# Coattention: the entry's own share of the output in float16 parts

## The reference, cut to what matters

```python
cq = einsum('bcd,bqd,d->bcq', c, q, w_cq) + b_cq
s = (c @ w_c + b_c)[:, :, None] + (q @ w_q + b_q)[:, None, :] + cq
a = softmax(s, axis=2)
c2q_att = einsum('bcq,bqd->bcd', a, q)
b_att = softmax(max(s, axis=2), axis=1)
q2c_att = einsum('bc,bcd->bd', b_att, c)[:, None, :]
x = concatenate([c, c2q_att, c * c2q_att, c * q2c_att], axis=-1)
z = x @ W_l.T + b_l          # added to the residual
```

## Time and profile before

| what | value |
|---|---|
| runs, median of 3 | 2402.48 us (2394.66 to 2403.4) |
| profiled execution | 2401.25 us |
| its span | 2399.5 us |
| TensorE busy in the span | 2083.1 us (87%) |
| VectorE, ScalarE, GpSimd busy | 1568.1, 1270.4, 1097.1 us |
| mean granted TensorE clock | 0.937 |

### The profile page before, as it was taken

One profiled execution on the slowest core, in us unless ns is written; L12 is line 12 of the kernel. 1 busy time (PEld: TensorE's weight loads), 2 busy tenths in 40 slices (PEclk: granted clock), 3 DMA queues, 4 the chain that ended last, 5 costly groups with the idle time before them and its releaser, 6 DMA issues. The chain is left out here.

```text
span 2399.5 us, 47249 instructions
## 1 busy us (share of the span) xinstructions
PE 2083.1 (87%) x17382; PEld 1468.1 (61%) x17382; DVE 1568.1 (65%) x3061; ACT 1270.4 (53%) x2058; POOL 1097.1 (46%) x1252
## 2 busy tenths in 40 slices
PE   7599999995887299967999969961999999999998
PEld 5466666663665177755666648841667667676675
DVE  5378888885897655547888746667555555555553
ACT  2266666664343166635666635532664664654653
POOL 2988888861221122226655314301545445455443
PEclk9799999997998599989999969985999999999999
DMA  5000000000002233311111000041434434434332
GB/s 226 1 2 1 0 0 0 0 1 6 8 9 71 77 130 114 114 44 32 32 30 26 0 11 18 15 141 69 114 75 110 105 80 109 101 101 100 87 78 30
DMA packets 66919, 136.00 MB, mean 57 GB/s; under 512 B 11201, under 2 KB 52369, under 8 KB 59921
## 3 DMA queue, kind: packets, MB, share of 16 engines
q1 hardware_dynamic: 37264, 87.65, 10.5%
q0 software_dynamic: 29568, 47.21, 10.0%
HBM read 100.22 MB, written 34.60 MB: 56 GB/s over the span
## 5 line engine op out<-in xcount | busy, mean ns | idle before, releaser
L3375 ACT ACTIVATE f_h<-bank,f_b 128x512 f32<-128x512 f32 x256 | 176.1, 688 | 275.6 <-PE bank L176 268.9
L3418 DVE TENSOR_TENSOR f_hidlo<-f_h,f_hidhi 128x512 f16<-128x512 f32 x256 | 177.1, 692 | 165.7 <-ACT f_hidhi L3376 161.9
L176 PE MATMUL ring<-f_w2hi,f_hidhi 128*128 128x256 f16 x1024 | 279.2, 273 | 5.9 <-DVE f_hidlo L3418 3.6
L176 PE MATMUL ring<-f_w2lo,f_hidhi 128*128 128x256 f16 x1024 | 279.1, 273 | 0.0
L176 PE MATMUL ring<-f_w2hi,f_hidlo 128*128 128x256 f16 x1024 | 279.1, 273 | 0.0
L3475 POOL DMA_INDIRECT out<-f_y,f_to_row x128 | 203.4, 1589 | 96.6 <-DVE f_y L3433 50.7
L176 PE MATMUL bank<-f_xthi,f_w1hi 128*128 128x512 f16 x512 | 194.6, 380 | 0.0
L176 PE MATMUL bank<-f_xtlo,f_w1hi 128*128 128x512 f16 x512 | 194.6, 380 | 0.0
L176 PE MATMUL bank<-f_xthi,f_w1lo 128*128 128x512 f16 x512 | 194.5, 380 | 0.0
L3376 ACT ACTIVATE f_hidhi<-bank,f_b 128x512 f16<-128x512 f32 x256 | 174.3, 681 | 0.0
L3460 POOL DMA_INDIRECT f_xg<-tokens,f_from_row x128 | 149.2, 1166 | 47.9 <-issue 34.6
(11 more groups left out here) (621 smaller groups left out, 6012.8 us busy)
## 6 DMA issues: line engine op xcount, KB each, us to landing
f_raw<-in_e_w SPq DMA_DIRECT2D x32, 1024.0 KB
c_raw<-in_e_w SPq DMA_DIRECT2D x16, 1024.0 KB, 5.1
slots_out<-c_y SPq DMA_DIRECT2D x40, 128.0 KB, 4.1
x<-in_x SPq DMA_DIRECT2D x1, 4096.0 KB
tokens<-c_xn SPq DMA_DIRECT2D x16, 256.0 KB, 2.7
tokens<-f_xn SPq DMA_DIRECT2D x16, 256.0 KB, 2.5
out<-x SPq DMA_DIRECT2D x1, 4096.0 KB, 14.3
wb<-in_wb SPq DMA_DIRECT2D x1, 3096.0 KB, 33.0
```

The costliest lines, as they stand in the source:

```text
L176: mm = pe.matmul(out, left[a], right[b], start=first and n == 0, stop=last and n == 2)
L3375: act.activation(h32[n % 4][:, :], src, ACT.Gelu_apprx_tanh, bias=bias).then_inc(sig["h_full"], 1)
L3418: dve.tensor_tensor(hid_v[1][:, it, at], h32[n % 4][:, :], hid_v[0][:, it, at], ALU.subtract).then_inc(sig["h_lo"], 1)
```

## The change

The product `k` = 2 becomes a `split_product` as well. Its operands need parts: ScalarE copies `xn_t` into a float16 high part, after the next pair's normalisation and before `c2q_t`; GpSimd subtracts it for the low part, between the bias and `cc_t`; ScalarE copies `w_eff` into a high part, as the last step of its turn; VectorE subtracts it for the low part, as the last step of its own, after the second twin's update. TensorE waits for the low part of `xn_t` and for that of `w_eff` ahead of the first `k` = 2 product of an entry. `w_eff` in float32 is no longer doubled by parity, its parts are. The declarations of the tiles are left out here.

```diff
@@ product (TensorE)
                     if t == 0 and k == 2:
-                        pe.wait_ge(u["w_eff_ready"], i.now)
+                        pe.wait_ge(u["xt_low_ready"], i.now)
+                        pe.wait_ge(u["w_eff_split"], i.now)
...
-                            mm = pe.matmul(out, u.xt_v[q][:, h, tok], u.we_v[q][:, h, :], start=False,
-                                           stop=h == KT - 1)
+                            mm = split_product(pe, out, [x[:, h, tok] for x in u.own_v[q][0]],
+                                               [w[:, h, :] for w in u.own_v[q][1]], False, h == KT - 1)
@@ pair (ScalarE)
                         norm(1 - q, Turn(i.now, None), i.before)
                     for u in twins:
+                        act.wait_ge(u["xn_t_ready"], i.now)
+                        act.activation(u.xt_parts[q][0][:, :], u.xn_t[q][:, :], ACT.Copy).then_inc(u["xt_high_ready"], 1)
+                    for u in twins:
                         act.wait_ge(u["c2q_made"], i.now)
...
                         act.activation(u.cc_parts[q][0][:, :], u.cc_t[q][:, :], ACT.Copy).then_inc(u["cc_high_ready"], 1)
+                    for u in twins:
+                        act.wait_ge(u["w_eff_ready"], i.now)
+                        act.activation(u.we_parts[q][0][:, :], u.w_eff[:, :], ACT.Copy).then_inc(u["w_eff_high"], 1)
@@ pair (GpSimd)
+                    for u in twins:
+                        pool.wait_ge(u["xt_high_ready"], i.now)
+                        pool.tensor_tensor(u.xt_parts[q][1][:, :], u.xn_t[q][:, :], u.xt_parts[q][0][:, :], ALU.subtract
+                                           ).then_inc(u["xt_low_ready"], 1)
                     for u in twins:
                         pool.wait_ge(u["c2q_ready"], i.now)
@@ pair (VectorE)
                     if ago is not None:
                         update(twins[1], ago)
+                    for u in twins:
+                        dve.wait_ge(u["w_eff_high"], i.now)
+                        dve.tensor_tensor(u.we_parts[q][1][:, :], u.w_eff[:, :], u.we_parts[q][0][:, :], ALU.subtract
+                                          ).then_inc(u["w_eff_split"], 1)
                     order.restart()
```

More of the change, by code:

```diff
@@ L2755, in coattention @@
             u.b_col, u.q2c, u.tmp = sb("b_col", NT), sb("q2c", KT), sb("tmp", W2)
[L2756 to L2759, removed]
+            u.xn, u.xn_t, u.c2q_t, u.cc_t = ([sb(f"{n}{q}_", W2) for q in range(2)]
+                                             for n in ("xn", "xn_t", "c2q_t", "cc_t"))
+            u.w_eff = sb("w_eff", W2)
+            u.cq_parts, u.cc_parts, u.xt_parts, u.we_parts = ([[ctx.enter_context(nc.sbuf_tensor(f"e_{n}_{part}{p}{q}", [P, W2], F16))
+                                        for part in ("hi", "lo")] for q in range(2)]
+                                                              for n in ("cq", "cc", "xt", "we"))
             u.c_v, u.sw_v = (tiles(t[:, :], KT) for t in (u.c_t, u.sim_w))
-            u.xt_v, u.we_v = ([tiles(t[:, :], KT) for t in both] for both in (u.xn_t, u.w_eff))
+            u.xt_v, u.we_v = [tiles(t[:, :], KT) for t in u.xn_t], tiles(u.w_eff[:, :], KT)
+            u.own_v = [[[tiles(t[:, :], KT) for t in parts[q]] for parts in (u.xt_parts, u.we_parts)] for q in range(2)]
             u.mid_v = [[[tiles(t[:, :], KT) for t in parts[q]] for parts in (u.cq_parts, u.cc_parts)] for q in range(2)]
@@ L3022, in pair @@
                         for h in range(KT):
-                            ins = dve.scalar_tensor_tensor(out=u.we_v[q][:, h, :], in0=w_l[:, 3, h, :],
+                            ins = dve.scalar_tensor_tensor(out=u.we_v[:, h, :], in0=w_l[:, 3, h, :],
                                                            scalar=u.q2c[:, h:h + 1], in1=w_l[:, 0, h, :], op0=ALU.mult,
```

## The result

The changed kernel takes 2426.15 us (median of 6 runs, 2420.69 to 2433.21) against 2402.68 us (median of 6, 2394.66 to 2405.68): ratio 1.0097, 95% interval 1.008 to 1.0113, so slower by about one per cent. The forecast was 2427.0. The profiled execution has a span of 2425.2 us at a mean clock of 0.931; before, 2399.5 at 0.937.

The account below looks back on a forecast made before the run. TensorE was taken as the bound. Seven turns at 2.3 (16.1) plus 2.0 for the tail make 18.1; with 8.4 of clock, 2401.25 becomes 2427.8, less about a microsecond for the first turn: 2427 us, range 2411 to 2437.

Parts of the forecast that it names:

- The wait on ScalarE: `w_eff`'s high part holds up the next turn's copies; similarity product 2.5 us later, a turn 2.3 us longer after 0.21 saved.
- `cq_lo` beside GpSimd: VectorE's `cq_lo` meets GpSimd's delayed `cc_lo`; costs about 0.6 us a turn, bounds 0 and 0.97.
- What was costed at nothing: ScalarE's two high-part copies of `xn_t` and VectorE's low part of `w_eff`, 1.28 us, were taken as covered.
- Only one of four savings counts: TensorE's own share saves 0.21 us four times a turn; only the one between similarity product and peaks' transposes surely shortens it.
- The tail: After the last turn TensorE waits for `w_eff`'s low part: 2.8 us late, 0.84 given back, 2.0 us.
- The clock: Idle stretches of 2.4 us a turn lower TensorE's clock in the tail and three turns, 2.1 us each: 8.4.
- The first turn: TensorE is at the lower clock there anyway, so it should pay about a microsecond less.
- clock kept: Rival: idle stretches prove too short to lower the clock, only the 18.1 us stand; about 2419; chance 0.28.
- Not slower: Rival: ScalarE gets `w_eff` in time through an earlier context transfer, savings show; 2395 to 2403 us; chance 0.12.

Follow-up runs that it names:

- the later high part: Changed kernel with ScalarE making the high part of `w_eff` behind the next turn's `xn_t` copies instead of ahead of them; 2420.25 us, ratio 1.0063 to the kernel before.
- GpSimd earlier: Changed kernel with `xn_t`'s high part right behind its copy on ScalarE, its low part on GpSimd once the second `e_a` is there; 2421.95 us, ratio 1.0085.
- the bias held back: Changed kernel with `w_eff`'s high part behind the next turn's copies, and GpSimd's bias waiting for the low parts of `w_eff`; 2412.45 us, ratio 1.0036.
- the filled run: Changed kernel with TensorE kept busy in the new waits by products whose result is overwritten; 2418.71 us, ratio 1.006 to the kernel before.
- the run with everything moved: Changed kernel with the parts of `xn_t` and `w_eff` made where engines were idle and own shares last among the pair's products; 2399.57 us, ratio 0.9992.

## Why the prediction was right

Most steps came out, and the sum nearer than they did, in part by luck. By the profile after, the start, the first turn and the clock in three turns cost 4.1 us more than forecast (1.7, 0.8 and 1.6); the six turns and the tail cost 1.5 less, and what lies outside the stage was 2.4 shorter, without an added instruction in it.

- **The wait on ScalarE (2.3 us a turn, the 0.6 of `cq_lo` in it).** Measured 2.15 at a full clock, from a similarity product 2.34 late (forecast 2.5) and 0.16 given back behind it (0.21). `w_eff` to similarity product took 3.17 us, forecast 3.2. Shown by undoing it alone: the later high part puts the similarity product back in its place, though another wait then keeps the turn long.
- **`cq_lo` beside GpSimd (0.6).** Measured 0.50, on an overlap of 0.64: most of the overlap, not the whole of it that the forecast counted. With GpSimd earlier, the turn is 0.5 shorter.
- **What was costed at nothing.** `xt_hi` twice is 1.13 us, and `c2q_t` follows without a wait, 3.82 us into the turn where it was 3.83. The low part of `w_eff` is free in the turns, as the run without it shows. The forecast's condition on this, that these 1.3 us would be the delay if the similarity product were on time, came true in the two runs with the later high part: 1.25 us with the bias held back, and twice that where they meet GpSimd's bias. I had the condition and did not use it when I forecast that run.
- **Only one of four savings counts (0.21).** 0.25 to 0.3 was measured. The wait for `e_a` did not grow by the next one, as the forecast had it; it stays at 0.33.
- **The tail (2.0, and 2.1 of clock).** Its wait is 3.64 (forecast 3.7); the whole part grew by 3.5, against 4.1. With the wait filled and the clock at 1.00 it grew by 2.0 (20.37, from the transposes at 1574.38 to the last product, against 18.36).
- **The clock (tail and three turns, 8.4).** The direction is shown by the filled run, which is 7.9 us faster for more work and has no fall behind its first turn. The count of three is luck: profiles of the changed kernel had three turns and one, the run without the low part five. The price was 1.6 to 3.2 us in the profile after, not 2.1. The step that failed is the reading of a border between 2.13 and 2.69 us of idle: falls followed 1.78 and, in the run with the later high part, 1.27; one of 2.39 was followed by none.
- **The first turn (1 us less than the others).** Wrong. It paid 2.1 and the start 1.7, with no wait for `e_xn_t` in either: in the profile before the clock was up for more of that stretch (0.78 and 0.73) than in the profile after (0.50 and 0.63). In one experiment, the later high part, the first turn took 18.97 us, in the other seven 20.7 to 23.1, of which 21.30 in the run with everything moved, whose later turns are shorter than before. With a single profile of before it stays open whether this is chance or belongs to the change.

Of the rivals, "clock kept" was 18.1 us over the kernel before, about 2419; the filled run, which holds the clock behind its first turn, was 13.9 over (that its 2418.71 comes so near is luck, as the kernel before took 2404.78 on its chip). "Not slower" needed `w_eff` earlier through the context's transfer; that wait stayed at 3.10 us (3.04 before). It could be had another way, by moving the work as the last run does.

## What to carry to other kernels

On an engine that takes its instructions in order, price a new wait by what stands behind it in the queue and who needs that, not by its own duration: here two copies of 0.63 us, behind a late `w_eff` and ahead of the next turn's copies, cost 1.6 of the 2.15 us a turn. When such a wait is moved, look again at which two-input VectorE and GpSimd instructions now coincide, since undoing one lateness can make another of its size. And where TensorE is the bound, count a new idle stretch twice, once as time and once as a possible loss of clock behind it (here 1.6 to 3.2 us a fall); harmless products in the gap tell the two apart.

## What was not expected of the hardware

The same program, with idle stretches of 1.8 to 2.4 us once a turn, had its clock lowered in one turn of one profile and in three of another, behind 1.78 us and not always behind 2.39. Its four runs spread over 15 us, the filled kernel's four over 2.9; that the falls make this spread fits but is not shown, as the kernel before spread over 8.5 without these stretches. What decides besides the length was not found. And most of what VectorE and GpSimd lose beside each other can fall on VectorE: two `we_lo`, 1.28 us together, lost 1.2 beside GpSimd's bias, which lost 0.44.
